# A graph kernel's weighted sums on VectorE: the loop written out, and the packed window word loaded between the additions

## The chip, the core and the metric

The kernel runs on one core of a Trainium2 chip. Its time is the device time of one execution in microseconds (us), and lower is better. A core has TensorE (PE; its weight loads are shown as PEld), VectorE (DVE), ScalarE (ACT), GpSimd (POOL) and SyncE (SP), which here only starts transfers. Each engine takes the instructions of its own program in order; they meet through semaphores. In the profile a name that ends in q, as DVEq, is the sequencer of that engine: it does the register arithmetic, the waits and the register loads, and hands the real work to the engine.

## The reference, cut to what matters

Two layers of a graph network run over 3125 nodes with 256 features and 50,000 edges, each with a residual and a layer norm. The change touches the last part of the second, a graph attention with 8 heads:

```python
ex = jnp.exp(alpha - amax[dst])
denom = jax.ops.segment_sum(ex, dst, num_segments=n)
attn = ex / jnp.maximum(denom[dst], 1e-10)
out = jax.ops.segment_sum(h_src * attn[..., None], dst, num_segments=n)
```

For every edge, the source row `h_src` is weighted with `ex` of its head, and the weighted rows are summed over the edges of each destination node. The kernel sums the 8 weights beside the 256 features, which gives `denom` in the same pass.

## The kernel before, in words

The edges are sorted by destination before this part. They lie in `NC` = 416 chunks of 128 edges, one edge to a partition, and each chunk belongs to one window of 128 nodes (there are at most 26). Four chunks are a quad, `NQ` = 104 of them, and four quads are a step b of `NB` = 26. The window numbers of a quad are packed, 5 bits each, in one integer of `quad_windows`, which lies in SBUF.

The weighted sums are made by five engines in a pipeline, quad after quad:

- SP loads the source rows of a quad into one of four slots of `gath` (L544, issued at L566 and L567 when the slot has been read).
- POOL multiplies them by the weights `s_sb` into one of four slots of `val` (L663).
- ACT makes the one-hot matrices that say which node of the window each edge belongs to: four `Square` (L1231, function `distances`) and one `Relu` (L1237, function `onehots`). `distances(g + 1)` waits until `onehots(g - 1)` is done, since they share a slot of `far`.
- PE multiplies one-hot by `val`, 264 columns to a chunk, two matmul instructions to a chunk (L1039, function `attend`). A chunk goes to one of eight banks of PSUM, so quad g waits until the sums of quad g - 2 have been added.
- DVE copies the weights into the last 8 columns of `val` (L1854, function `exp_columns`, one reduce to a quad) and adds each chunk's 264 columns from PSUM to its window's row of `acc` or `x0`, by turns (L1848, function `add`). Which row that is comes from a register: `windows` (L409 to L415) loads the packed word of the quad from SBUF into a register (L410) and takes the four window numbers out of it with shifts and masks (L414).

On PE, ACT, POOL and DVE the steps in the middle are a hardware loop (`Fori`), with some of the first and last steps written out. On DVE `sum_chunks` (L1857) does for each quad: the reduce of a quad two ahead, then load and take apart the word of the quad, then its four additions. The loop L1872 runs over b = 1 to 24; the quads 0 to 2 and 99 to 103 are added by straight-line code. Within the loop the waits of `add` (L1844, L1846) are for values that depend on b, so they too are computed in registers.

Behind this, from L1879 on, DVE adds `x0` to `acc` in one instruction (L1880), divides, and computes the layer norm; the output follows.

Of the kernel before, what the change touches and what calls it, by code (L numbers as in the profile page):

```python
# [23 lines left out]
NW = 26  # L24
# [34 lines left out]
NC = 416  # L59
NCD = NC + 16  # L60
NB = NC // 16
NQ = NC // 4
# [9 lines left out]
WBITS = 5  # L72
# [10 lines left out]
def build(nc, x, src, dst, edge_attr, edge_weight, Wn, bn, Ws, bs, W, a_src, a_dst, edge_W, edge_b, bias, out):  # L83
    with ExitStack() as ctx:
# [42 lines left out]
        def carve(at, shape, dt=F32):  # L127
            n = int(np.prod(shape)) * (2 if dt == BF16 else 4) // 4
            v = digits[:, at:at + n]
            if dt != F32:  # L130
                v = v.bitcast(dt)
            if len(shape) == 2:
                v = v.rearrange("p (a b) -> p a b", b=shape[1])
            if len(shape) == 3:
                v = v.rearrange("p (a b c) -> p a b c", b=shape[1], c=shape[2])
            return v, at + n

        digit, q = carve(0, [EC, 2], BF16)
        rk, q = carve(q, [EC])
        rk_i, q = carve(q, [3, SEGS, MID], I32)  # L140
        begin, q = carve(q, [4, DIG])
        begin_i, q = carve(q, [2, DIG], I32)
        oh = carve(q, [4, HS, DIG], BF16)[0]
        keep, q = carve(q, [DIG, SEGS])
        picked = carve(q, [2, HS, DIG])[0]
        totals, q = carve(q, [DIG, SEGS])
        seed, q = carve(q, [2, HS, DIG])
        summed, q = carve(q, [DIG, SEGS])
# [257 lines left out]
        def nodes(t):  # L406
            return t.rearrange("(w p) d -> p w d", p=P)

        def windows(engine, g, n=1):  # L409
            words = nc.values_load_multi_w_load_instructions(  # L410
                quad_windows[0:1, bass.ds(g, n)], engines=(engine,), min_val=0, max_val=(1 << 4 * WBITS) - 1,
                skip_runtime_bounds_check_because="four counts of the USED windows, less one, of WBITS bits each")[1]
            eng = {mybir.EngineType.PE: nc.tensor, mybir.EngineType.DVE: nc.vector}[engine]
            return [eng.compute_val((word >> WBITS * j) & (1 << WBITS) - 1).with_bounds(min_val=0, max_val=NW - 1)  # L414
                    for word in words for j in range(4)]  # L415

        def split(eng, parts, full, sem_, q):
            for i in range(3):
# [271 lines left out]
        def _(pe):  # L690
# [274 lines left out]
            def score(b, p0, first, second):  # L965
                for q in range(4):
                    g = 4 * b + q
                    if q % 2 == 0:
                        ws = windows(mybir.EngineType.PE, g, 2)
# [295 lines left out]
        def _(dve):  # L1265
# [377 lines left out]
            for k in range(HOPS):  # L1643
                for g in range(NG):
                    n = k * NG + g
# [135 lines left out]
            last, firstm, k0, k1, cont, sing, p_, o_ = (el[:, i, :] for i in range(8))  # L1781
# [61 lines left out]
            def add(n, k, w):  # L1843
                dve.wait_ge(s_mm, n + 1)  # L1844
                if not (isinstance(n, int) and n < 2):
                    dve.wait_ge(s_add, n - 1)  # L1846
                a = (acc, x0)[k % 2][:, bass.ds(w, 1), :].rearrange("p c d -> p (c d)")
                v.tensor_tensor(a, a, bank[k][:, 0:HX], ALU.add).then_inc(s_add, 1)  # L1848


            def exp_columns(g, q, first):
                if not first:
                    dve.wait_ge(s_mm, 4 * (g - 3))
                v.tensor_reduce(val[:, q, :, D:HX], s_sb[:, bass.ds(4 * g, 4), :].unsqueeze(3), X,  # L1854
                                ALU.max).then_inc(s_vx, 1)

            def sum_chunks(b, first, last):  # L1857
                for q in range(4):
                    g = 4 * b + q
                    if not (last and q >= 2):  # L1860
                        exp_columns(g + 2, (q + 2) % 4, first and q < 2)
                    if not (first and q == 0):
                        ws = windows(mybir.EngineType.DVE, g - 1)
                        for j in range(4):
                            add(4 * (g - 1) + j, 4 * ((q + 1) % 2) + j, ws[j])

            dve.wait_ge(s_exs, len(quads))
            exp_columns(0, 0, True)
            exp_columns(1, 1, True)
            dve.wait_ge(s_clr, 2)  # L1870
            sum_chunks(0, True, False)
            with dve.Fori(1, NB - 1) as b:  # L1872
                sum_chunks(b, False, False)
            sum_chunks(NB - 1, False, True)
            ws = windows(mybir.EngineType.DVE, NQ - 1)
            for j in range(4):
                add(NC - 4 + j, 4 + j, ws[j])

            dve.wait_ge(s_add, NC)  # L1879
            v.tensor_tensor(acc[:, :, :], acc[:, :, :], x0[:, :, :], ALU.add).then_inc(s_add, 1)  # L1880
# [67 lines left out]
```

## Time and profile before

| | us |
|---|---|
| median of 3 runs | 3014.15 |
| lowest and highest of them | 3014.09, 3016.46 |
| the profiled execution, its own time | 3018.76 |
| its span, from the first to the last instruction | 3016.7 |
| of it, from the first `Square` of the weighted sums to L1880 | 2706.2 to 2971.8 |

| engine | busy in the whole span, us | share |
|---|---|---|
| PE | 2460.3 | 82% |
| POOL | 1855.6 | 62% |
| DVE | 1722.3 | 57% |
| ACT | 1073.7 | 36% |

Register, branch, semaphore and DMA-issuing instructions are not counted as busy. "Idle before" a row is time in which its engine did no counted work, and the name behind the arrow is what is inferred to have ended it, from the semaphore event that came last.

### The profile page before, as it was taken

Reading aid. Unit: us, or ns where it says so; the run is one execution under the profiler, and the core shown is the slowest. Engines: PE = TensorE matmul, PEld = TensorE weight load, DVE = VectorE, ACT = ScalarE, POOL = GpSimd, SP = SyncE. Lnnn points to the kernel's source line nnn. Section 1 sums busy time; section 2 is a strip of 40 time slices with the busy share of each in tenths; the row PEclk is TensorE's granted clock in tenths of the full one; section 3 lists DMA queues with packets and bytes.
Section 4 is the critical chain, followed back from the end, with each engine's and each line's share of the span. In section 5 each row is a group of like instructions: output and inputs, shape, how many; then the busy total and the mean of one; then the engine's idle time right before and its main releaser. Section 6 shows DMA issues by size and latency. Waiting matters only on the chain.

```text
span 3016.7 us, 48565 instructions
## 1 busy us (share of the span) xinstructions
PE 2460.3 (82%) x9398; PEld 1569.3 (52%) x9399; DVE 1722.3 (57%) x4280; ACT 1073.7 (36%) x3018; POOL 1855.6 (62%) x1739
## 2 busy tenths in 40 slices
PE   6999976477777779999899999999776767738883
PEld 5888853255555544445444454445554545525552
DVE  7765558799999940001334411103777777766667
ACT  1222221398888840000000000000333333338773
POOL 4777777777777770000057777770577777757774
PEclk9999979699999999999999999999788888869997
DMA  4000000255555565443344444543477777747772
GB/s 128 3 4 3 3 25 3 99 183 183 184 184 184 184 196 152 129 132 110 101 122 121 128 115 128 143 134 106 141 217 218 218 217 218 217 132 230 215 212 85
DMA packets 425652, 415.45 MB, mean 138 GB/s; under 512 B 85386, under 2 KB 411489, under 8 KB 424929
## 3 DMA queue, kind: packets, MB, share of 16 engines
q1 hardware_dynamic: 367681, 348.28, 36.9%
q0 software_dynamic: 57888, 66.23, 9.4%
q8 instruction: 32, 0.52, 0.1%
q14 instruction: 51, 0.42, 0.0%
HBM read 247.08 MB, written 167.17 MB: 137 GB/s over the span
## 4 chain that ended last, share of the span: by engine, by line
PE 37%; POOL 23%; issue 15%; SPq 10%; DVE 6%; DMA 4%; DVEq 3%; ACT 1%; ACTq 0%; POOLq 0%
PE psum L923 27%; POOL rows_by_pair L608 13%; POOL gath L647 10%; SPq L497 7%; PE psum L1039 2%; PE psum L915 2%; DMA gath<-gat_rows,rec 2%; SPq L491 2%; PE psum L794 1%; DMA adjacency<-merged 1%; PE psum L883 1%; PE psum L853 1%; DVE acc L1848 1%; DVEq L414 1%; DVE x L1848 1%
## 5 line engine op out<-in xcount | busy, mean ns | idle before, releaser
L633 POOL DMA_INDIRECT rows_by_dst<-rec,place x392 | 382.6, 976 | 534.0 <-DVE place L1468 405.9
L923 PE MATMUL psum<-a_t,acc 128*128 128x512 f32 (+1 forms) x1400 | 553.7, 551 | 0.0
L647 POOL DMA_INDIRECT gath<-gat_rows,rec x416 | 404.6, 973 | 213.0 <-issue 117.1
L618 POOL DMA_INDIRECT rows_by_low_digit<-rec,place x392 | 437.6, 1116 | 127.7 <-issue 127.7
L853 PE MATMUL psum<-rhot,lw 128*128 128x256 f32 x1440 | 381.8, 419 | 162.7 <-ACT lw L1110 124.3
L608 POOL DMA_INDIRECT rows_by_pair<-rec,place x392 | 389.0, 992 | 159.5 <-issue 126.7
L853 PEld LDWEIGHTS psum<-rhot,lw 128*128 128x128 f32 x1440 | 276.4, 206 | 268.1 <-ACT lw L1110 170.7
L923 PEld LDWEIGHTS psum<-a_t,acc 128*128 128x128 f32 x1400 | 257.3, 195 | 272.1 <-issue 268.3
L1576 DVE SCALAR_TENSOR_TENSOR merged<-merged,same_of,psum 128x256 f32<-128x256 f32 x720 | 309.7, 476 | 30.4 <-PE psum L853 18.7
L923 PE MATMUL psum<-a_t,x 128*128 128x512 f32 (+1 forms) x700 | 294.3, 549 | 0.0
L1110 ACT ACTIVATE lw<-lhot,recs_pair 128x128 f32<-128x128 bf16 x720 | 236.8, 387 | 98.6 <-DVE lhot L1559 87.8
L994 PE MATMUL psum<-x,acc 128*128 x832 | 258.5, 458 | 5.1 <-DVE acc L1715 4.4
L1039 PE MATMUL psum<-ht 128*128 128x264 f32 x832 | 214.2, 402 | 48.8 <-DVE acc L1848 45.2
L663 POOL TENSOR_TENSOR ht<-gath,digits 128x1024 f32<-128x1024 f32 x104 | 198.7, 1914 | 64.9 <-PE psum L1039 56.8
L1039 PEld LDWEIGHTS psum<-ht 128*128 128x128 f32 x832 | 151.1, 191 | 111.9 <-DVE acc L1848 86.0
L735 PEld LDWEIGHTS psum<-table,ohhiT 32*128 32x128 f32 x784 | 181.1, 318 | 53.2 <-issue 33.7
L994 PEld LDWEIGHTS psum<-x,acc 128*128 128x128 f32 x832 | 180.0, 231 | 50.6 <-issue 16.9
L735 PE MATMUL psum<-table,ohhiT 32*128 32x16 f32 x784 | 202.2, 375 | 1.4 <-issue 1.2
L1659 DVE TENSOR_SCALAR et<-et 128x512 f32<-128x512 f32 (+1 forms) x28 | 11.0, 394 | 334.0 <-ACT et L1138 333.8
L1715 DVE TENSOR_TENSOR acc<-wT,psum 128x528 f32<-128x528 f32 x208 | 145.2, 698 | 94.7 <-issue 41.8
L923 PEld LDWEIGHTS psum<-a_t,x 128*128 128x128 f32 x700 | 126.2, 191 | 114.0 <-issue 109.0
L1345 DVE SCALAR_TENSOR_TENSOR terms<-psum,kst,earlier 128x128 f32<-128x128 f32 (+1 forms) x392 | 139.8, 412 | 44.8 <-PE psum L720 34.3
(322 smaller groups left out, 3392.9 us busy)
## 6 DMA issues: line engine op xcount, KB each, us to landing
a_t<-adjacency SPq DMA_DIRECT2D x450, 256.0 KB, 2.7
adjacency<-merged SPq DMA_DIRECT2D x721, 128.0 KB
gat_h_by_edge<-gath SPq DMA_DIRECT2D x104, 528.0 KB, 4.2
gath<-gat_h_by_edge SPq DMA_DIRECT2D x104, 528.0 KB, 3.9
gath<-gat_rows,rec POOLq DMA_INDIRECT x416
rows_by_pair<-rec,place POOLq DMA_INDIRECT x392
rows_by_low_digit<-rec,place POOLq DMA_INDIRECT x392
rows_by_dst<-rec,place POOLq DMA_INDIRECT x392
```

The costliest lines, as they stand in the source:

```text
L497: sp.dma_start(adj[bass.ds(to[j], 1), :, :].rearrange("b p c -> p (b c)"), merged[:, j, :]).then_inc(s_st[j], 16)
L608: pool.indirect_dma_start(out=rows_pair, in_=rec[:, c, :], out_offset=bass.IndirectOffsetOnAxis(ap=place[:, 0, c:c + 1], axis=0), in_offse ...
L618: pool.indirect_dma_start(out=rows_low, in_=rec[:, c, :], out_offset=bass.IndirectOffsetOnAxis(ap=place[:, 1, c:c + 1], axis=0), in_offset ...
L633: pool.indirect_dma_start(out=rows_dst, in_=rec[:, c, :], out_offset=bass.IndirectOffsetOnAxis(ap=place[:, 0, c:c + 1], axis=0), in_offset ...
L647: pool.indirect_dma_start(out=gath[:, g % 4, c % 4, :], out_offset=None, in_=hh_dram, in_offset=bass.IndirectOffsetOnAxis(ap=rec_i[:, c, 0 ...
L735: pe.matmul(bank[7 * s][:, j * LO:(j + 1) * LO], ohhiT[:, 4 * s + j, :], table[:, half, :], start=True, stop=True, skip_group_check=True). ...
L853: pe.matmul(bank[j % 4][:, 0:SW], lw[:, p, j, :], rhot[:, p, j, :], start=True, stop=True).then_inc(s_bmm, 1)
L923: i = pe.matmul(sums[b], table_g[:, w, b * P:(b + 1) * P], a_t[:, q % NA, 0:width(g)], start=False, stop=w == USED - 1)
L994: i = pe.matmul(bank[4 + j][:, 0:HX], ohT[:, q % 2, j * P:(j + 1) * P], x0[:, bass.ds(ws[4 * (q % 2) + j], 1), :].rearrange("p c k -> p (c ...
L1039: pe.matmul(bank[4 * (q % 2) + j][:, 0:HX], onehot[:, q // 2, 4 * (q % 2) + j, :], val[:, q, j, :], start=True, stop=True).then_inc(s_mm, 1)
L1110: nc.scalar.activation(lw[:, p, j, :], lhot[:, p, j, :], ACT.Copy, scale=recs_pair[:, bass.ds(at, 1), 2]).then_inc(s_lw, 1)
L1576: v.scalar_tensor_tensor(out=merged[:, j, :], in0=merged[:, (j - 2) % U, :], scalar=same_of[:, bass.ds(s, 1)], in1=bank[j % 4][:, 0:SW], o ...
```

## The change

`windows` is cut into two functions, one that loads the packed word and one that takes one window number out of it; PE goes on using the whole. On DVE, `sum_chunks` and its loop go away: the 104 quads are written out. The first three reduces and the load of word 0 come ahead; then each quad does its first addition, the reduce of the quad three ahead, the load of the next quad's word, one window number of the next quad, and then by turns an addition and the next window number. What is computed is the same.

```diff
+        def window_word(engine, g, n=1):
+            return nc.values_load_multi_w_load_instructions(
                 quad_windows[0:1, bass.ds(g, n)], engines=(engine,), min_val=0, max_val=(1 << 4 * WBITS) - 1,
                 skip_runtime_bounds_check_because="four counts of the USED windows, less one, of WBITS bits each")[1]
+
+        def window_of(eng, word, j):
+            return eng.compute_val((word >> WBITS * j) & (1 << WBITS) - 1).with_bounds(min_val=0, max_val=NW - 1)
...
-            def sum_chunks(b, first, last):
-                for q in range(4):
-                    g = 4 * b + q
-                    if not (last and q >= 2):
-                        exp_columns(g + 2, (q + 2) % 4, first and q < 2)
-                    if not (first and q == 0):
-                        ws = windows(mybir.EngineType.DVE, g - 1)
-                        for j in range(4):
-                            add(4 * (g - 1) + j, 4 * ((q + 1) % 2) + j, ws[j])
-
             dve.wait_ge(s_exs, len(quads))
-            exp_columns(0, 0, True)
-            exp_columns(1, 1, True)
+            for g in range(3):
+                exp_columns(g, g, True)
+            ws = windows(mybir.EngineType.DVE, 0)
             dve.wait_ge(s_clr, 2)
-            sum_chunks(0, True, False)
-            with dve.Fori(1, NB - 1) as b:
-                sum_chunks(b, False, False)
-            sum_chunks(NB - 1, False, True)
-            ws = windows(mybir.EngineType.DVE, NQ - 1)
-            for j in range(4):
-                add(NC - 4 + j, 4 + j, ws[j])
+            for g in range(NQ):
+                later = []
+                for j in range(4):
+                    add(4 * g + j, 4 * (g % 2) + j, ws[j])
+                    if j == 0:
+                        if g + 3 < NQ:
+                            exp_columns(g + 3, (g + 3) % 4, g == 0)
+                        if g + 1 < NQ:
+                            word = window_word(mybir.EngineType.DVE, g + 1)[0]
+                    if g + 1 < NQ:
+                        later.append(window_of(nc.vector, word, j))
+                ws = later
```

## Rows read from the trace of the kernel before

**Rows 1.** Windows view, steady stretch: busy us (x instructions), clock, DMA share, GB/s.
```profile
core 0: us, PE busy (x) PEld busy (x) DVE busy (x) ACT busy (x) POOL busy (x), PEclk, DMA share, GB/s
2740.00:2960.00 220.00, 178.14 (x696) 124.72 (x696) 136.45 (x437) 173.60 (x435) 166.59 (x87) 1.00 0.70 209
```

**Rows 2.** Waits, 2745 to 2960: who waited for whom, us in total, times, longest.
```profile
DVE acc L1848 <- PE psum L1039: 80.9, 86, 1.1
...
POOL ht L663 <- PE psum L1039: 51.9, 85, 0.9
PE psum L1039 <- DVE acc L1848: 40.6, 85, 0.7
ACT ht L1237 <- PE psum L1039: 34.3, 86, 1.8
```

**Rows 3.** Timeline of DVE, quad 3, one loop quad, quad 99: start us, us, idle before.
```profile
2719.79 0.43 DVE L1848 TENSOR_TENSOR acc<-acc,psum 128x264 f32 x1 [1.06 <-PE psum L1039]
...
2803.21 0.43 DVE L1848 TENSOR_TENSOR acc<-acc,psum 128x264 f32 x1 [0.94 <-PE psum L1039]
...
2804.58 0.18 DVE L1854 TENSOR_REDUCE ht<-digits 128x32 f32 x1
2805.69 0.43 DVE L1848 TENSOR_TENSOR acc<-acc,psum 128x264 f32 x1 [0.93 <-PE psum L1039]
...
2961.87 0.43 DVE L1848 TENSOR_TENSOR acc<-acc,psum 128x264 f32 x1 [0.70 <-PE psum L1039]
```

**Rows 4.** Chain of waits through the same quad: start us, us, what.
```profile
2804.55 0.21 DVEq L410
...
2804.89 0.04 DVEq L414
2804.93 0.03 issue
2804.96 0.04 DVEq L414
...
2805.40 0.04 DVEq L1844
```

**Rows 5.** Instructions of L410 and L414: count, ns min/median/max, first and last start.
```profile
L414 DVEq ALU_OP  x7: 45/45/45, 2804.9 to 2805.3; - x7
...
L410 DVEq TENSOR_LOAD <-quad_windows x104: 300/304/557, 2706.2 to 2969.3; - x104
...
L410 PEldq TENSOR_LOAD <-quad_windows x52: 537/1128/1640, 2143.0 to 2647.1; - x52
```

**Rows 6.** Timeline of DVE, straight-line quads without a reduce, and L1880.
```profile
2965.24 0.42 DVE L1848 TENSOR_TENSOR x<-x,psum 128x264 f32 x1
2966.26 0.43 DVE L1848 TENSOR_TENSOR acc<-acc,psum 128x264 f32 x1 [0.60 <-PE psum L1039]
...
2968.31 0.43 DVE L1848 TENSOR_TENSOR acc<-acc,psum 128x264 f32 x1 [0.60 <-PE psum L1039]
...
2971.38 0.42 DVE L1848 TENSOR_TENSOR x<-x,psum 128x264 f32 x1
2971.84 7.31 DVE L1880 TENSOR_TENSOR acc<-acc,x 128x6864 f32<-128x6864 f32 x1
```

**Rows 7.** Timeline of ACT, L1237 for quads 2, 3, 4, 17, 18; last its count, 3 to 17.
```profile
2712.39 0.70 ACT L1237 ACTIVATE ht<-wT,ones 128x512 f32<-128x512 f32 x1
...
2714.31 0.71 ACT L1237 ACTIVATE ht<-wT,ones 128x512 f32<-128x512 f32 x1
...
2716.35 0.70 ACT L1237 ACTIVATE ht<-wT,ones 128x512 f32<-128x512 f32 x1
...
2742.81 0.71 ACT L1237 ACTIVATE ht<-wT,ones 128x512 f32<-128x512 f32 x1
...
2745.11 0.72 ACT L1237 ACTIVATE ht<-wT,ones 128x512 f32<-128x512 f32 x1 [0.17 <-PE psum L1039]
...
L1237 ACT ACTIVATE ht<-wT,ones x15: 705/707/708, 2714.3 to 2742.8; 128x512 f32<-128x512 f32 x15
```

**Rows 8.** POOL's timeline and PE's matmuls while nothing held them up.
```profile
2715.78 11.28 POOL L663 TENSOR_TENSOR ht<-gath,digits 128x1024 f32<-128x1024 f32 x6
...
L1039 PE MATMUL psum<-ht x31: 386/386/386, 2715.6 to 2722.3; 128*128 128x264 f32 x31
```

**Rows 9.** Windows view of that stretch, and its loads of rows: us to landing.
```profile
2710.00:2727.00 17.00, 16.51 (x64) 12.98 (x62) 9.82 (x30) 16.07 (x43) 16.85 (x10) 0.87 0.94 280
...
DMA to landing us min/median/max: 4.2/4.9/5.3
```

**Rows 10.** Waits of DVE in straight-line code, the scores before the sums, 2200 to 2600.
```profile
DVE acc L1715 <- issue: 37.9, 18, 2.8
```

## What the change is predicted to do

> **What bounds the kernel now.** I read the stage of the weighted sums alone, since the change touches nothing else; it ends with L1880, and what follows starts from there. The windows view comes first: in 220 us no engine is full. PE is busy 178, ACT 174, POOL 167 and DVE, on which the others wait, only 136 [rows 1]. The table of waits gives a ring: PE waits for DVE's additions, POOL and ACT wait for PE, and DVE is said to wait for PE, 86 times and 80.9 us [rows 2]. A ring has one member that isn't really waiting. The timeline shows which: the additions of a quad start 0.34 us apart, the reduce starts at 2804.58 and runs 0.18, then DVE idles 0.93 until 2805.69 [rows 3]. The chain through the same quad fills this hole with sequencer work: the load of the word at 2804.55, seven shifts and masks from 2804.89 to 2805.40, then the wait values and the address [rows 4]. PE is named only because its event is the last one on record. So DVE's sequencer sets the pace: 2.48 us for this quad, and over the loop, from the step to the next, 2.52 (2719.79 for quad 3 to 2961.87 for quad 99 is 242.1 us, over 96; the fourth quad of a step also carries the branch) [rows 3]. Straight-line quads without a reduce take 2.05 (2966.26 to 2968.31) [rows 6].
>
> **The change, part by part.**
>
> *The load.* It takes 0.30 us (median 304 ns) [rows 5]. Does it wait for work that DVE has in hand? In the loop it starts at 2804.55, before the reduce that was issued ahead of it has even started (2804.58) and while the last addition runs [rows 3, 4]. So behind the first addition and the queued reduce it should run beside both.
>
> *The window numbers.* Seven operations, 0.07 us apart [rows 4, 5], 0.52 in all. They are not fewer, but now one stands behind the load and two behind each of the other additions.
>
> *The fixed cost of an addition.* In straight-line code the way from the last addition of a quad to the first of the next is 1.02 us (2965.24 to 2966.26) [rows 6]. Less 0.30 for the load and 0.52 for seven operations, 0.20 remain for a wait, an address and the gaps. The register arithmetic for wait values (L1844) [rows 4] and the loop's branch go away.
>
> *The new pace of DVE alone.* From the first addition to the second: 0.06 until the load starts, 0.30, one operation 0.07, then 0.20, with a gap 0.03: 0.66. The engine itself would be free after 0.34 + 0.10 for the reduce. The other three steps: a gap of 0.03, two operations 0.15, 0.20: 0.38 against the engine's 0.34. Sum 0.66 + 3 x 0.38 = 1.80 us a quad. From both sides: with all register work free the engine needs 4 x 0.34 + 0.10 = 1.46; if nothing is overlapped it is the straight-line 2.05 plus a reduce of 0.18, 2.23 [rows 3, 6]. I take 1.80, because the rows show both the load and the shifts running while an addition is under way.
>
> *Of the load the trace and a page differ.* The 104 loads on DVE took 300 to 557 ns, median 304 [rows 5]. The Trainium skill, page "DMA: Bandwidth & Descriptors", section "Latency and other measured facts", gives a load of this name a floor of about 600 ns. By the page the quad would be 0.3 us longer, about 2.1, and I go by the row. That is the first rival below, with a price from rows.
>
> **What is late next.** With DVE at 1.80 the pace is set by the slowest of the others, and the first 30 us show each running free, because DVE's lag had not yet filled the buffers:
> - PE: 31 matmuls start from 2715.6 to 2722.3, 0.223 apart, so 1.78 a quad [rows 8].
> - POOL: six quads in 11.28, (11.28 - 1.91) / 5 = 1.87 [rows 8].
> - ACT: L1237 of quad 3 starts at 2714.31, of quad 17 at 2742.81, with no idle time before any: 28.50 / 14 = 2.036 a quad in its loop, branch included, and 1.92 (2712.39 to 2714.31) in its straight-line part [rows 7]. Four `Square`, then the `Relu`, and the next `Square` waits for that `Relu`.
> - The loads of rows: POOL's free stretch had them at share 0.94 and 280 GB/s, landing in 4.9 us, at most 5.3 [rows 9]. A slot leaves three quads of time. At 2.04 a quad that is 6.1 us, and the share is 0.70 x 2.52 / 2.04 = 0.87 [rows 1]. They hold.
>
> So ACT becomes the bound, at 2.036. Nothing of its first 18 quads moves, as DVE never held it there. The stage then ends thus: L1237 of quad 99 starts at 2714.31 + 96 x 2.036 = 2909.8; quads 100 to 102 are straight-line, 3 x 1.92, 2915.5; its end 2916.2. PE does the quads 102 and 103 from 2916.25 in 16 x 0.223 = 3.57, then 0.16 until the last is out and 0.15 to the addition: 2920.1. It runs 0.42, and L1880 starts at 2920.6 in place of 2971.84 [rows 6]. The gain is **51.2 us**. The first reduces and word 0 are issued while PE still waits for its first one-hots, so they cost nothing. What follows L1880 is the same DVE work, also straight-line, and I take no change there.
>
> The profiled execution took 3018.76 (2.1 more than its span), so its like would take 2967.5. The median of the runs shown is 4.6 lower than it: 3014.15 - 51.2 = **2963**.
>
> **The rivals.**
>
> *A, DVE stays the bound.* The load or the overlap costs more than I take. With a load of 0.6 us DVE needs 1.80 + 0.30 = 2.10 a quad; from quad 3 at about 2719, 100 quads end at 2929, some 1.5 us more until L1880: 41 us saved, 2973. With nothing overlapped, 2.23 a quad: 28 saved, 2986. For it: the margin between 1.80 and 2.036 is only 0.24 us a quad. Against it: the load that began beside a queued reduce [rows 3, 4].
>
> *B, straight-line code has to be fetched.* A loop of four quads runs from what is there; 104 written-out quads don't. The nearest row is the straight-line scores, where DVE lost 37.9 us in 18 waits to nothing that the profile names [rows 10]. If all that were fetching and came again, DVE would need 100 x 1.80 + 38 = 218 from 2719, ending near 2938.5: 33 saved, 2981. Against it: the last quads, straight-line at 2.05, show exactly the sum of their register work and no hole. The Trainium skill, page "Runtime: NRT & Kernel Launch", section "Instruction fetch mechanics", says that sequential fetch is mostly hidden and that taken branches are what breaks it; that speaks against B, and no row here prices one fetch.
>
> *C, slower.* The load between the additions waits until the engine is empty or the SBUF read gets through. On PE's queue the same load took 537 to 1640 ns, median 1128 [rows 5]. In place of 0.30, the median gives 1.80 + 0.83 = 2.63 a quad, and 100 quads from 2719 end at 2982, L1880 at 2983.5: 11 us slower, 3025; with 1640 it is 3.14 and 63 slower. It decides from a load of about 1.02 us on. Against it: all 104 loads on DVE were below 0.56.
>
> *D, no change.* The named wait is real: DVE does wait for PE, and early registers gain nothing, 3014. Against it: PE's matmuls of the quad end well before the addition, and PE itself waits for DVE 40.6 us [rows 2].
>
> **How the numbers follow.** Forecast 0.78, A 0.10, B 0.04, C 0.04, D 0.04. A measurement of this kernel can tell 0.2%, 6 us, from no change; the forecast, A and B are all faster by more, so faster 0.92, same 0.04, slower 0.04. The range reaches from 2958, for an error of 5 us in my pace of ACT and in the offset of profile and median, to 2978, which takes in A with a load of 0.6 us.
>
> **What would show it.** In the changed kernel's trace: L1880 starts near 2920.6; L1237 on ACT goes through all 104 quads 2.04 apart with no idle time before it; the load starts within 0.1 us of a quad's first addition, and the second addition comes 0.6 to 0.7 behind the first; PE's idle time is ended by ACT's L1237 and not by L1848; POOL and ACT hardly wait for PE. If PE still waits for L1848 in each quad and ACT for PE, DVE is the bound still and A or C holds; the distance of the first two additions tells which. If holes of a microsecond or more come at even distances in DVE's instructions, it is B. The prediction is wrong if the stage's pace is above 2.1 us or below 2.0.

## The result, and the profile after

The changed kernel takes 2963.81 us (median of 4 runs, 2961.12 to 2964.15), against 3014.97 for the kernel before in the same comparison: ratio 0.9828, 95% interval 0.9811 to 0.9845. A later comparison gave 2964.53 against 3014.72, 0.9832 (0.9815 to 0.9848). The forecast was 2963.

I measure the stage from POOL's first product (L663 before, L667 after) to the start of L1880. It was 2706.24 to 2971.84, 265.6 us. It is now 2701.4 to 2915.9, 214.5, so it is 51.1 shorter. The other 4.8 us between the spans of 3016.7 and 2960.8 lie outside the stage, in code that is the same; over the profiled executions on chips like this one what lies outside took 2744.3 to 2751.2.

The windows view of the stage (after; columns as in [rows 1]):

```profile
core 0: us, PE busy (x) PEld busy (x) DVE busy (x) ACT busy (x) POOL busy (x), PEclk, DMA share, GB/s
2740.00:2900.00 160.00, 159.96 (x630) 113.00 (x629) 132.18 (x395) 148.62 (x394) 150.62 (x80) 1.00 0.89 267
```

and its table of waits, 2745 to 2900 (who waited for whom, us in total, times, longest):

```profile
PEld psum L1043 <- DVE x L1852: 29.4, 73, 0.4
DVE acc L1852 <- PE psum L1043: 13.0, 56, 0.6
...
POOL ht L667 <- PE psum L1043: 1.3, 7, 0.2
```

The ring of [rows 2] is gone: ACT isn't in the table, POOL's 51.9 us are 1.3, and DVE's 80.9 are 13.0. PE reads as full. That is a trap, as ACT's rows below show. One quad and the start of the next on DVE in steady state, for [rows 3]:

```profile
2802.77 0.43 DVE L1852 TENSOR_TENSOR acc<-acc,psum 128x264 f32 x1 [0.21 <-PE psum L1043]
2803.12 0.18 DVE L1858 TENSOR_REDUCE ht<-digits 128x32 f32<-128x32 f32 x1
2803.43 0.43 DVE L1852 TENSOR_TENSOR x<-x,psum 128x264 f32 x1
2803.79 0.43 DVE L1852 TENSOR_TENSOR acc<-acc,psum 128x264 f32 x1
2804.16 0.43 DVE L1852 TENSOR_TENSOR x<-x,psum 128x264 f32 x1
2804.81 0.43 DVE L1852 TENSOR_TENSOR acc<-acc,psum 128x264 f32 x1 [0.22 <-PE psum L1043]
```

A quad takes 2.04 in place of 2.48, and the second addition comes 0.66 behind the first. Now ACT's one-hots, as in [rows 7], over all 104 quads (count, ns min/median/max, first and last start), and in time:

```profile
L1241 ACT ACTIVATE ht<-wT,ones x104: 704/707/711, 2703.7 to 2911.3; 128x512 f32<-128x512 f32 x104
```

```profile
2803.10 0.71 ACT L1241 ACTIVATE ht<-wT,ones 128x512 f32<-128x512 f32 x1
2803.95 1.28 ACT L1235 ACTIVATE wT<-iota_f,lo_s 128x128 f32<-128x128 f32 x4
2805.14 0.71 ACT L1241 ACTIVATE ht<-wT,ones 128x512 f32<-128x512 f32 x1
2805.99 1.27 ACT L1235 ACTIVATE wT<-iota_f,lo_s 128x128 f32<-128x128 f32 x4
```

The view of L1241 lists no idle time before any of the 104. ACT is "busy" 149 of 160 us, less than PE or POOL, and is the bound all the same: the 0.14 us between the end of a Relu (2805.85) and the next Square (2805.99) is no work and no wait that the view counts. PE's sequencer resumes right when that Relu ends, with the instruction that waits for the semaphore that the Relu raises (the record bears the line of the wait beside it):

```profile
L1042 PEldq FUSED_REGOPS x1: 42/42/42, 2805.9 to 2805.9; - x1
```

PE's 8 matmuls of a quad need 1.78 of the 2.04; the modelled end of the last one covers the gap, so that no idle time shows. The loads of rows land later than before (median 3.9 there) and at most just use up the 6.1 us that they have; twice POOL waited for one, 0.6 us in all. 2740 to 2900:

```profile
DMA to landing us min/median/max: 3.7/4.7/6.1
```

And the stage's first free stretch, where DVE still had a backlog and ran by itself, shows its own pace and one thing that the forecast left out:

```profile
2717.43 0.43 DVE L1852 TENSOR_TENSOR acc<-acc,psum 128x264 f32 x1
...
2719.18 0.43 DVE L1852 TENSOR_TENSOR acc<-acc,psum 128x264 f32 x1
...
2722.70 0.43 DVE L1852 TENSOR_TENSOR acc<-acc,psum 128x264 f32 x1
...
2723.73 0.43 DVE L1852 TENSOR_TENSOR acc<-acc,psum 128x264 f32 x1
2724.45 0.43 DVE L1852 TENSOR_TENSOR x<-x,psum 128x264 f32 x1 [0.29 <-DVE acc L1852]
2724.81 0.43 DVE L1852 TENSOR_TENSOR acc<-acc,psum 128x264 f32 x1
```

A quad takes 1.755 (2717.43 to 2722.70, three quads), but the one from 2722.70 to 2724.81 takes 2.11: one addition comes 0.72 behind the last in place of 0.36. Such a hole comes every sixth quad.

### The profile page after: what moved, and what is told of

It reads as the page before. It is cut to its first block, busy times and chain, and to the rows that moved or that the text cites. A ratio compares the mean times of both kernels' runs of the same rounds, so it can differ in the third digit from the quotient of the medians.

```text
span 2960.8 us, 47868 instructions
## 1 busy us (share of the span) xinstructions
PE 2453.8 (83%) x9398; PEld 1569.8 (53%) x9399; DVE 1735.3 (59%) x4279; ACT 1062.9 (36%) x3018; POOL 1850.7 (63%) x1739
## 4 chain that ended last, share of the span: by engine, by line
PE 52%; POOL 16%; issue 11%; SPq 9%; DVE 5%; DMA 5%; ACT 1%; DVEq 0%; ACTq 0%; POOLq 0%
PE psum L927 27%; POOL gath L651 9%; PE psum L1043 7%; POOL rows_by_pair L612 7%; SPq L501 7%; PE psum L739 4%; DMA gath<-gat_rows,rec 3%; PE psum L724 2%; PE psum L919 2%; SPq L495 2%; PE psum L798 1%; PE psum L857 1%; DMA adjacency<-merged 1%; PE psum L715 1%; PE psum L887 1%
## 5 line engine op out<-in xcount | busy, mean ns | idle before, releaser
L667 POOL TENSOR_TENSOR ht<-gath,digits 128x1024 f32<-128x1024 f32 x104 | 198.0, 1914 | 18.3 <-ACT digits L1229 7.8
```

## The experiments

Ten of these ran on chips where the kernel before itself took 4259 to 4266 us. The 1250 us more lie outside the stage, whose length in the changed kernel was 214.5 on every chip, in four traces (e3's among them). The kernel with both edits to ACT varied more, 197.9 to 199.8 in three. So I compare stages and give the ratio to the kernel before in the same comparison beside them.

| run | stage, us | us a quad (quads 24 to 96) | ratio to before (95%) |
|---|---|---|---|
| before | 265.6 | 2.526 | |
| changed | 214.5 | 2.036 | 0.9828 (0.9811 to 0.9845) |
| e0, changed | 214.5 | 2.035 | 0.9869 (0.9852 to 0.9887) |
| e1, written out, old order | 227.3 | 2.137 | 0.9888 (0.9862 to 0.9915) |
| e2, new order, in the loop | 253.8 | 2.419 | 0.9970 (0.9955 to 0.9984) |
| e3, second load unused | 214.5 | 2.035 | 0.9874 (0.9851 to 0.9897) |
| e7, two loads | 229.5 | 2.155 | 0.9917 (0.9900 to 0.9933) |
| e9, three loads | 263.9 | 2.492 | 1.0002 (0.9990 to 1.0014) |
| e4, ACT written out | 203.8 | 1.924 | 0.9856 (0.9834 to 0.9877) |
| e6, four slots of far | 198.8 | 1.875 | 0.9844 (0.9825 to 0.9863) |
| e5, ACT written out and four slots | 197.9 | 1.870 | 0.9848 (0.9832 to 0.9863) |
| e10, the same as e5 | 199.8 | 1.883 | 0.9854 (0.9838 to 0.9870) |
| e11, changed, on a chip like the first | 214.5 | 2.035 | 0.9832 (0.9815 to 0.9848) |
| e12, the same as e5, on the chip of e11 | 198.1 | 1.874 | 0.9776 (0.9759 to 0.9792) |

The us a quad are those of PE's first matmul of a quad.

**The two halves of the change.** e1 writes the loop out and keeps the order of before (only the reduce between two quads is for a quad one earlier than before):

```diff
             for g in range(NQ):
-                later = []
+                if g:
+                    ws = windows(mybir.EngineType.DVE, g)
                 for j in range(4):
                     add(4 * g + j, 4 * (g % 2) + j, ws[j])
...
+                if g + 3 < NQ:
+                    exp_columns(g + 3, (g + 3) % 4, g == 0)
```

> Only half of the change: the 104 quads are written out on DVE, but in the order of before (load of the word, seven shifts and masks, four additions, reduce). My theory: register work sets DVE's pace, and straight-line code alone takes away the wait arithmetic and the branch. In the old tail a quad with its reduce took 1.02 us over three steps and 1.07 from the last addition to the next quad's first, so 2.10, and the holes of 0.35 us that the changed kernel shows every six quads add 0.06: 2.15 a quad, just above ACT's 2.036. DVE stays the bound, ending about 10 us later than the changed kernel: 2974 us. Rival, that the loads between the additions are what counts: near 2.4 a quad and 3005 us. Rival, that the loop alone was the cost: 2964 us, ACT idle nowhere.

The stage was 227.3: 38.3 of the 51.1 us come from writing out alone. That is 12.8 more than the changed kernel's, where about 10 were expected. The first theory holds and both rivals fall. Its DVE:

```profile
4018.11 0.43 DVE L1852 TENSOR_TENSOR acc<-acc,psum 128x264 f32 x1 [0.54 <-PE psum L1043]
...
4020.20 0.43 DVE L1852 TENSOR_TENSOR acc<-acc,psum 128x264 f32 x1 [0.54 <-PE psum L1043]
...
4021.57 0.18 DVE L1858 TENSOR_REDUCE ht<-digits 128x32 f32<-128x32 f32 x1
4022.65 0.43 DVE L1852 TENSOR_TENSOR acc<-acc,psum 128x264 f32 x1 [0.91 <-PE psum L1043]
```

The first of these quads takes 2.09 (4018.11 to 4020.20), and DVE's idle time in it is 0.54 in place of the 0.93 of [rows 3]: the arithmetic for the wait values and for the addresses of the reduce and of the load is gone, the load and the seven shifts are still there. The next quad holds a hole, 0.91. e2 is the other half, the new order within each step of the loop:

```diff
+            def step(b, head, tail):
+                ws = windows(mybir.EngineType.DVE, 4 * b) if not head else first_ws
+                for q in range(4):
+                    ws = quad(4 * b + q, q, ws, head and q == 0, head, tail)
...
+            with dve.Fori(1, NB - 1) as b:
+                step(b, False, False)
```

where `quad` is the changed kernel's body, without loading a word in a step's last quad.

> The other half: the loop over b stays on DVE, and within each step of four quads the next word is loaded and taken apart between the additions; only the first word of a step is taken apart with nothing beside it. My theory: three quads at about 2.17 us (1.75 as in the changed kernel, and some 0.1 more at each of four waits computed in registers), the fourth at 1.5 with 1.1 behind it for the branch, the load and seven shifts: 9.1 us a step, 2.28 a quad, 2990 us. Rival, that interleaving alone brings all: 2.04 a quad, 2964 us. Rival, that the loop is all the cost: no gain, 3014 us.

It gained 11.8 us. Both rivals fall, and my size was off: 2.42 a quad in place of 2.28. The rows show where it went:

```profile
4053.00 0.43 DVE L1852 TENSOR_TENSOR acc<-acc,psum 128x264 f32 x1 [1.23 <-PE psum L1043]
4053.34 0.18 DVE L1858 TENSOR_REDUCE ht<-digits 128x32 f32 x1
4053.96 0.43 DVE L1852 TENSOR_TENSOR x<-x,psum 128x264 f32 x1 [0.44 <-issue]
4054.40 0.43 DVE L1852 TENSOR_TENSOR acc<-acc,psum 128x264 f32 x1
4054.84 0.43 DVE L1852 TENSOR_TENSOR x<-x,psum 128x264 f32 x1
4055.30 0.43 DVE L1852 TENSOR_TENSOR acc<-acc,psum 128x264 f32 x1
```

The first step costs 0.96, since in a loop the addresses of the reduce and of the load depend on b and are computed too, and the others 0.44, with one more operation (0.07) for each wait. The registers' work that stands between additions is no longer covered by the engine's 0.34, so in a loop the new order gives a quad only 0.18 (2.48 to 2.30). Without the loop it gives 0.33 (2.09 to 1.755).

**Does the register load cost its whole time?** e3 loaded the word twice and used one.

> The changed kernel with one more load of the same word right before the other, its value unused. My theory: DVE runs a quad in 1.755 us by itself with a hole of 0.35 us every six quads, 1.81; one load more, about 0.33 us with its gap, makes it 2.14, above ACT's 2.036, so the second addition comes 1.0 us behind the first, DVE becomes the bound again and the kernel is some 10 us slower than the changed one: 2974 us. The slack of 0.23 us a quad would be shown from above. Rival, that DVE has more slack than that, since the load runs beside the reduce: 2964 us. The holes should come after fewer quads, since each has one instruction more (22 in place of 21).

It tests nothing: the trace holds the same 47,868 instructions as the changed kernel's, so the unused load was dropped, and neither its theory nor its rival was tried. What it does show is that the stage repeats, 214.5. e7 keeps a copy of the words and uses both loads, e9 has three:

```diff
-                            word = window_word(mybir.EngineType.DVE, g + 1)[0]
+                            both = [window_word(mybir.EngineType.DVE, g + 1, of=t)[0] for t in (None, quad_copy)]
...
-                        later.append(window_of(nc.vector, word, j))
+                        later.append(window_of(nc.vector, both[j // 2], j))
```

> The changed kernel with two loads to a quad that both count: the word lies in SBUF twice (one small copy on DVE before the sums), window numbers 0 and 1 come from one load, 2 and 3 from the other, right behind it. My theory, in the length of the stage from POOL's first product to L1880, which was 214.5 us: DVE alone 1.755 + about 0.34 for the second load, and a hole of 0.35 every six quads, 2.15 a quad, above ACT's 2.036. The second addition comes 1.0 us behind the first, DVE is the bound and the stage is 11 us longer, 226. Rival, that the load hides beside the reduce and costs nothing: 214.5.

> The same with three loads to a quad, each from a copy of its own. My theory: past the slack of 0.23 us a quad, each load costs its whole 0.34: 2.49 a quad, the stage 34 us longer again than with two, about 260, which is nearly the length before the change (265.6). It is the price at which the change would have gained nothing, 1 us of loads between two additions, as in the third rival of the prediction. Rival, that more loads pipeline behind each other: 235 or less.

Two loads made the stage 229.5, three 263.9, each about 4 us more than expected. The second addition, here with two:

```profile
4052.15 0.18 DVE L1859 TENSOR_REDUCE ht<-digits 128x32 f32<-128x32 f32 x1
4052.82 0.43 DVE L1853 TENSOR_TENSOR x<-x,psum 128x264 f32 x1 [0.49 <-PE psum L1044]
```

and with three:

```profile
4051.50 0.43 DVE L1854 TENSOR_TENSOR acc<-acc,psum 128x264 f32 x1
4051.85 0.18 DVE L1860 TENSOR_REDUCE ht<-digits 128x32 f32<-128x32 f32 x1
4052.85 0.43 DVE L1854 TENSOR_TENSOR x<-x,psum 128x264 f32 x1 [0.82 <-PE psum L1045]
```

It comes 0.66, 1.00 and 1.34 behind the first: 0.34 for each load, none of it hidden by the next, and the quads without a hole take 1.755, 2.094 and 2.433. The first extra load costs the stage only 15.0 us, because 0.23 of its 0.34 is slack below ACT's pace (with holes, 2.036 - 1.81). That accounts for 8.9 us from quad 24 to quad 96. Another 5.0 fall before quad 24, which the expectation left out: there the changed kernel's DVE still works off the backlog of the stage's start, and with two loads it can't. The next load costs 34.4, its whole price times 104. With three the gain of the change is gone, ratio 1.0002. The rows with idle time name PE as what the addition waited for. It was the sequencer, since the delay grows by one load's time with each load and PE's work is the same.

**Who is the bound now?** ACT alone is changed. e4 writes its loop out:

```diff
-            attend(0, True, False)
-            with act.Fori(1, NB - 1) as b:
-                attend(b, False, False)
-            attend(NB - 1, False, True)
+            for b in range(NB):
+                attend(b, b == 0, b == NB - 1)
```

> The changed kernel with ACT's one-hot loop written out too. My theory: ACT is the new bound at 2.036 us a quad, and its straight-line quads took 1.92, so 96 x 0.114 = 11 us go: 2953 us. Rival, that DVE, PE or the loads of rows at the higher rate bind as tightly: 2960 us or more.

e6 gives `far` four slots in place of two, with the loop as it is:

```diff
-        far = late[:, 0:8 * P].rearrange("p (s c d) -> p s c d", s=2, c=4)
+        far = late[:, 0:16 * P].rearrange("p (s c d) -> p s c d", s=4, c=4)
...
-                        if not (first and q == 0):
-                            act.wait_ge(s_oneh, g)
+                        if not (first and q < 3):
+                            act.wait_ge(s_oneh, g - 2)
```

> The changed kernel with ACT's loop as it is, but four slots of far in place of two, so that the Squares of the next quad needn't wait for the Relu before them. My theory: ACT's pace falls from 2.036 to its own work, four Squares 0.29 apart and a Relu of 0.71, about 1.8 to 1.9, and POOL at 1.874 takes over as the bound: 96 x 0.16 = 15 us less than the changed kernel, 2949 us. Rival: the wait for the Relu is hidden and ACT stays at 2.036: 2964 us.

> Both: ACT written out and four slots of far. My theory: POOL at 1.874 us a quad is the bound with either, so this gives the same 2949 us as the four slots alone; POOL shows almost no idle time in the stage. Rival: the loads of rows can't keep up at share 0.94 and POOL waits for them: 2955 us. Rival: DVE with its holes, 1.81, or PE at 1.78 binds through the ring: also above 2949.

> The changed kernel unaltered, as the measure for the other three on the same chip: 2964 us by every theory.

The stage fell by 10.7, 15.7 and 16.6 us, where 11, 15 and 15 were expected. So PE, full by the windows view, wasn't the bound, and ACT was. With four slots the Square no longer waits for the Relu before it, and ACT by itself needs 1.78 a quad, here in e6, loop and all:

```profile
4001.04 0.71 ACT L1241 ACTIVATE ht<-wT,ones 128x512 f32<-128x512 f32 x1
4002.82 0.71 ACT L1241 ACTIVATE ht<-wT,ones 128x512 f32<-128x512 f32 x1
```

That is off the bound, and POOL's 1.874 shows: e6 and e5 both sit at 1.87, whether ACT's loop is written out or not. In whole time these three can't be told apart on that chip (0.9844 to 0.9856), and hardly from the changed kernel (e0, 0.9869, whose interval overlaps all three); the stages tell them apart. The kernel of e5 twice more, the second time with the changed kernel beside it:

> ACT written out and four slots of far once more, as the candidate for the fastest. In the stage 197.9 us as in its first run, against 214.5 of the changed kernel and 265.6 before; so 68 us less than before the change in all, 2946 us where the kernel before takes 3014.

> The changed kernel unaltered, as the measure beside the next one: stage 214.5 us by every theory, and 51 us less than the kernel before.

> ACT written out and four slots of far, a third time: the stage 198 to 200 us, and the whole 15 us less than the changed kernel, since what is changed lies on the path throughout. Rival: whole times lie closer than the stages do, because something behind the stage waits; then L1880 starts 15 us earlier but the end moves by less.

e10's stage was 199.8 us in place of the 197.9 expected: POOL stood idle once for 1.05 us (at 4117.02), and why PE was late there stays open. e12 took 2946.33 us (2944.14 to 2949.09), beside 2964.53 for the changed kernel and 3014.72 for the one before on the same chip: ratio to before 0.9776 (0.9759 to 0.9792). It beats both. The 18.2 us less are the stage's 16.4 and the spread outside; the rival of a later wait falls. Its stage:

```profile
2740.00:2880.00 140.00, 139.64 (x601) 108.02 (x600) 124.04 (x376) 139.41 (x384) 139.52 (x76) 1.00 0.95 288
```

```profile
L667 POOL TENSOR_TENSOR ht<-gath,digits x104: 1904/1914/1928, 2699.4 to 2892.7; 128x1024 f32<-128x1024 f32 x104
```

POOL works back to back, 1.877 from one start to the next (2699.4 to 2892.7 over 103), and the transfers stand at share 0.95. That POOL is the bound is read from these rows; no run changed POOL or the transfers. With both eased, DVE's 1.81 with holes would be next, so about 0.07 us a quad is left there.

## Why the prediction was right

- **DVE's sequencer sets the pace before.** Shown: the additions come earlier when register work is taken away (e1) or moved between them (e2) and later by exactly what is put in (e7, e9), with PE, ACT and POOL untouched. That the wait was charged to PE was a matter of the last event. The rival of a real wait for PE falls.
- **The load runs beside the addition and the queued reduce, at 0.30 us.** The second addition was put at 0.66 behind the first and came at 0.66. The floor of about 600 ns (the Trainium skill, page "DMA: Bandwidth & Descriptors", section "Latency and other measured facts") isn't what DVE pays: 104 loads took 298 to 554 ns, median 304, and an additional one costs 0.34 in e7 and e9. The measurement decides. Had the page's figure held, 0.30 more, the kernel would by my estimate have been close to e7, whose stage is 15 us longer.
- **DVE alone at 1.80.** It is 1.755 without a hole, 1.81 with. The three other steps are 0.365 and not 0.38. The number was right because two small errors cancel: I saw no holes.
- **ACT is late next, at 2.036.** Shown by e4 and e6. The sum over ACT's rows put L1880's start 51.2 us earlier; the stage is 51.1 shorter. That the whole time came within 1 us of the forecast is in part luck: what lies outside the stage varied by 7 us over four executions, and in the changed kernel's trace L1880 starts at 2915.9, not at 2920.6, because the stage itself began 4.8 us earlier.
- **Straight-line code has to be fetched.** There are such holes, at a sixth of the 38 us that I gave them: 0.35 us every sixth quad, 17 of them, 6 us of DVE's time, and in the steady state within its slack. They come at even distances, as the rival's sign said, but the sign asked for a microsecond or more. In e1, e7 and e9, where DVE is the bound, they cost 0.05 to 0.06 us a quad (2.137 against 2.086 and so on).
- **Slower from about 1.02 us of loads on.** Three loads take 0.30 + 2 x 0.34 = 0.98 us, and e9 is level with the kernel before. The threshold was right, the condition false.
- **One sign was wrong.** I said that PE's idle time would be ended by ACT. PE shows none, and its weight loads are charged to DVE 73 times. Who read only that view would have called PE, or DVE still, the bound.

Not foreseen was how the gain splits. Writing out takes DVE from 2.53 to 2.14 a quad, the order from there to 1.81; of that second step only 0.10 counts, as ACT stops it at 2.036.

## What to carry to other kernels

When engines wait for each other in a ring, follow the chain through the sequencers: here the engine whose idle time was filled with register loads and shifts was the bound, whatever the wait was charged to. The register load behind an issued instruction ran beside it; put such a load and the shifts where the engine still has queued work, and count the loop's own branch and arithmetic for waits and addresses, which here was three quarters of the gain. Before such a change, read the pace at which every other engine ran while the buffers were still filling: here it told the next bound and with it the gain.

## What the runs showed of the hardware

**The holes.** With 21 sequencer and engine instructions to a quad, one hole of 0.35 us falls every sixth quad (2722.70, then 2.11 us for the quad where its neighbours take 1.755). The instruction queue moved 15 packets more than before, each of about 8 KB:

```profile
q14 instruction: 66, 0.54, 0.1%
```

where the kernel before shows 51 packets and 0.42 MB. Counted in the traces, the holes, where they can be seen, lie 128 of DVE's instructions apart, the sequencer's included, whether a quad has 21 of them (e1 and the changed kernel), 22 (e7) or 23 (e9). In e1 they start at 3970.11, 3983.12, 3996.15 and 4009.15, and 2.0 to 2.4 us behind each a packet of 8192 bytes starts on this queue. So a hole goes with each new packet of DVE's instructions; why it takes 0.35 us stays open.

The Trainium skill, page "Runtime: NRT & Kernel Launch", section "Instruction fetch mechanics", calls the cost of crossing a block mostly hidden and the block 16 KiB; the trace has a visible 0.35 us and packets of 8 KB in this queue.

**Other chips.** Where the kernel before took some 4260 us, matmuls in the sorting stages are followed by long stretches that nothing explains (waits in the changed kernel, e0: us in total, times, longest):

```profile
PEld psum L780 <- issue: 444.3, 73, 42.1
```

On the first chip this row isn't among the longest waits. The mean granted clock of the whole run was 0.826 in e0 and 0.928 on the first chip. The weighted sums, where PE works almost without a pause, took 214.5 us on either kind. What causes the difference stays open; no run was made for it.
